# A six-stage transformer kernel: norms by columns, last turns written out, six chunks of five batches in the first expert stage, five carried batches, a count of four products

## The reference

```python
x = x + 0.5 * ffn(layernorm(x))          # weights replaced by alpha * sign(w), gelu between, hidden 512
x = x + gau(layernorm(x))                # gated attention: groups of 32, a quadratic and a linear part
x = x + 0.5 * ffn(layernorm(x))
x = x + 0.5 * moe(layernorm(x))          # 8 experts, top 2, capacity 76 rows per batch and expert
x = x + lin(layernorm(x))                # linear attention, 16 heads of 64, sigmoid gate
x = x + 0.5 * moe(layernorm(x))
```

## Time and profile before

| | us |
|---|---|
| median of three runs | 2459.9 (2459.01 to 2463.73) |
| the profiled execution, its own time | 2451.63 |
| its span | 2449.7 |
| TensorE busy | 2261.4 (92%) |
| VectorE busy | 1594.4 (65%) |
| ScalarE busy | 1306.4 (53%) |
| GpSimd busy | 720.0 (29%) |
| setup, ffn, gau, ffn | 0 to 31.4, to 155.4, to 390.0, to 512.7 |
| moe, lin, moe | to 1063.8, to 1879, to 2449.7 |

### The profile page before, as it was taken

How to read it: one execution, slowest core, us unless ns; L and a number is a source line. 1 busy time by engine, 2 the same in 40 slices (tenths; PEclk the granted TensorE clock), 3 DMA queues, 4 the chain that set the end, 5 groups by cost and what they waited for, 6 DMA issues and landing times.

```text
span 2449.7 us, 48056 instructions
## 1 busy us (share of the span) xinstructions
PE 2261.4 (92%) x14882; PEld 1811.5 (74%) x14882; DVE 1594.4 (65%) x5061; ACT 1306.4 (53%) x2705; POOL 720.0 (29%) x814
## 2 busy tenths in 40 slices
PE   3979998968999999969999999999997889999996
PEld 3969997967766767757778787777776776667676
DVE  5877776776667766566565656565656666676754
ACT  3755555744444444446666666666663444444443
POOL 1202220024547665430000000000000356565654
PEclk9989999989999999999999999999998999999998
DMA  7040000000011111110000000000000001111122
GB/s 256 0 163 0 0 0 0 0 2 18 24 32 42 33 40 37 48 34 0 0 0 0 0 0 0 0 0 0 0 0 0 12 23 36 43 47 48 42 55 73
DMA packets 71011, 67.98 MB, mean 28 GB/s; under 512 B 9712, under 2 KB 58352, under 8 KB 70512
## 3 DMA queue, kind: packets, MB, share of 16 engines
q1 hardware_dynamic: 61648, 47.68, 6.2%
q0 software_dynamic: 8192, 16.79, 3.1%
q10 hardware_dynamic: 1056, 2.10, 0.3%
HBM read 32.47 MB, written 34.08 MB: 27 GB/s over the span
## 4 chain that ended last, share of the span: by engine, by line
PE 49%; DVE 3%; issue 2%; ACT 1%; POOL 0%; DMA 0%; ACTq 0%; POOLq 0%; DVEq 0%
PE moe_bank L1628 6%; PE moe_bank L1614 5%; PE lin_bank L1008 5%; PE moe_bank L1618 5%; PE lin_bank L934 5%; PE lin_bank L942 4%; PE lin_bank L953 4%; PE lin_bank L961 4%; PE lin_bank L984 4%; PE lin_bank L1000 2%; PE moe_bank L1602 2%; PE lin_bank L971 1%; ACT lin_xT L1071 0%; DVE all_x L1455 0%; POOL all_landed L1446 0%
## 5 line engine op out<-in xcount | busy, mean ns | idle before, releaser
L1692 ACT ACTIVATE moe_fc<-moe_bank,all_b_fc 128x380 f32<-128x380 f32 (+2 forms) x512 | 262.8, 513 | 312.6 <-PE moe_bank L1614 299.0
L1804 DVE SCALAR_TENSOR_TENSOR moe_act<-moe_bank,all_b_moe_gate,moe_fc 128x380 f32<-128x380 f32 (+2 forms) x512 | 270.4, 531 | 203.5 <-PE moe_bank L1618 113.3
L1618 PE MATMUL moe_bank<-moe_rowsT,all_w_gate 128*128 128x380 f32 (+2 forms) x1024 | 348.7, 422 | 6.9 <-DVE moe_act L1804 6.9
L1614 PE MATMUL moe_bank<-moe_rowsT,all_w_fc 128*128 128x380 f32 (+2 forms) x1024 | 353.9, 427 | 0.0
L1628 PEld LDWEIGHTS moe_bank<-all_w_proj,moe_act 128*128 128x128 f32 x2688 | 316.7, 193 | 12.4 <-ACT moe_act L1699 1.8
L1628 PE MATMUL moe_bank<-all_w_proj,moe_act 128*128 128x128 f32 x2688 | 324.5, 277 | 1.4 <-ACT moe_act L1699 1.4
L1446 POOL DMA_INDIRECT all_landed<-rows_out,all_take_at x256 | 266.5, 1041 | 128.7 <-issue 126.9
L1618 PEld LDWEIGHTS moe_bank<-moe_rowsT,all_w_gate 128*128 128x128 f32 x1024 | 185.9, 190 | 94.9 <-DVE moe_act L1804 9.6
L1524 POOL TENSOR_SCALAR moe_hot<-all_slot_ids,moe_slot 128x608 bf16<-128x608 f32 x120 | 219.3, 1835 | 85.8 <-issue 51.5
L1171 POOL COPY lin_xn_ones<-lin_xn 128x254 f32<-128x254 f32 x32 | 12.8, 400 | 741.0 <-PE lin_bank L942 737.6
L1699 ACT ACTIVATE moe_act<-moe_act 128x760 f32<-128x760 f32 (+2 forms) x256 | 181.5, 709 | 91.1 <-DVE moe_act L1804 91.0
(11 more groups left out here) (219 smaller groups left out, 4410.8 us busy)
## 6 DMA issues: line engine op xcount, KB each, us to landing
rows_out<-moe_expert_out SPq DMA_DIRECT2D x80, 128.0 KB
rows_out<-all_zeros SPq DMA_DIRECT2D x1, 9728.0 KB, 28.0
rows_out<-moe_expert_out SPq DMA_DIRECT2D x80, 62.0 KB
all_landed<-rows_out,all_take_at POOLq DMA_INDIRECT x256, 2.7
out<-all_x SPq DMA_DIRECT2D x5, 640.0 KB
rows_out<-moe_expert_out SPq DMA_DIRECT2D x48, 64.0 KB
...
```

The source lines that it names most:

```text
L1614: nc.tensor.matmul(bank[FC + j % 2][:, 0:c.width], k.w_fc[:, e, j * P:(j + 1) * P], rowsT[:, c.n % 2, e, 0:c.width], start=True, stop=True ...
L1618: nc.tensor.matmul(bank[GATE + j % 2][:, 0:c.width], k.w_gate[:, e, j * P:(j + 1) * P], rowsT[:, c.n % 2, e, 0:c.width], start=True, stop= ...
L1692: nc.scalar.activation(fc[:, j, 0:c.width], bank[FC + j % 2][:, 0:c.width], ACT.Identity, bias=k.b_fc[:, e * MC + j:e * MC + j + 1]).then_ ...
L1804: nc.vector.scalar_tensor_tensor(act_in[:, i % 2, j, 0:c.width], bank[GATE + j % 2][:, 0:c.width], k.b_moe_gate[:, e * MC + j:e * MC + j + ...
```

## The change

Six parts.

1. Setup: ScalarE issues its two parts of `x` only once the feed-forward weights have landed. VectorE takes the statistics of the first 16 tiles alone.
2. Norms: the form without ScalarE everywhere. The first 8 columns are computed first, then work begins, and the others follow after a few instructions of the stage. In `gau` both roots are computed together, in instructions of twice the width. In the first `ffn` stage the statistics of the other 48 tiles are taken there: 16 of them in the prologue, three in each of the first 12 turns, the last six after those; then follow the remaining 42 columns of the norm.
3. The last four turns of `ffn` and the last two of `gau` are written out without the work past batch 31.
4. The first `moe` stage uses chunks of (2, 5, 5, 5, 5, 5, 5), so chunk 0 routes five batches, at every fourth step. The last stage keeps its chunks and steps.
5. Five batches (27 to 31) are carried into `lin`, all gathered there by GpSimd. The first is combined before turn 0, the others at the ends of turns 0 to 3, which are written out; then 20 columns of the norm, then the loop.
6. `count` is four products instead of seven.

```diff
                 sp.dma_start(w2[:, 0, :], d["w2"]).then_inc(w_in, 16)
                 for i in range(2):
-                    sp.dma_start(k.x[:, 16 * i:16 * i + 16, :], xv[:, 16 * i:16 * i + 16, :]).then_inc(x_in[i], 16)
+                    sp.dma_start(k.x[:, X_PART * i:X_PART * (i + 1), :], xv[:, X_PART * i:X_PART * (i + 1), :]).then_inc(k.x_in[i], 16)
...
+                act.wait_ge(w_in, 48)
                 for i in range(2, 4):
...
-                act.wait_ge(w_in, 48)
...
-                for i in range(4):
-                    dve.wait_ge(x_in[i], 16)
-                    for t in range(16 * i, 16 * i + 16):
-                        last = nc.vector.bn_stats(k.stats[:, t, :], k.x[:, t, :])
+                dve.wait_ge(k.x_in[0], 16)
+                for t in range(X_PART):
+                    last = nc.vector.bn_stats(k.stats[:, t, :], k.x[:, t, :])
...
@@ ffn_stage, VectorE
-                norm.vector(dve)
+                norm.columns(dve, 0, FIRST)
...
+                def raw_stats(lo, n):
+                    for t in range(n):
+                        last = nc.vector.bn_stats(k.stats[:, lo + t, :], k.x[:, lo + t, :])
+                    return last
...
+                def turn(b, s, more=4):
+                    if more >= 4:
+                        normalise(b, 4, s)
+                    if more >= 3:
+                        split_rest(b, 3, 1 - s)
+                    add_out(b)
+                    if more >= 3:
+                        low_part(b, 3, 1 - s)
+                    add_bias(b)
...
                 normalise(0, 3, 1)
-                with dve.Fori(0, BATCHES, 2) as b:
+                norm.columns(dve, FIRST, known)
+                begun = 0
+                if first:
+                    begun = 12
...
+                    with dve.Fori(0, begun, 2) as b:
+                        for s in range(2):
+                            turn(b + s, s)
+                            raw_stats((b + s) * 3 + known, 3)
+                    raw_stats(known + 3 * begun, X_TILES - known - 3 * begun).then_inc(late, 1)
+                    dve.wait_ge(late, 2)
+                    norm.columns(dve, known, X_TILES)
+                with dve.Fori(begun, BATCHES - 4, 2) as b:
...
@@ ffn_stage, TensorE
-                with pe.Fori(0, BATCHES, 2) as b:
+                with pe.Fori(0, BATCHES - 4, 2) as b:
...
+                for b in range(BATCHES - 4, BATCHES):
+                    if b + 1 < BATCHES:
+                        up(b, 1, 1 - b % 2)
+                    if b + 3 < BATCHES:
+                        transpose(b, 3, 1 - b % 2)
+                    down(b, b % 2)
...
@@ gau_stage, VectorE
                 normalise(0, 0)
+                residual_scales(0, FIRST, 2)
+                norm.columns(dve, FIRST, X_TILES)
                 split_heads(0, 0, 0)
...
@@ lin_stage, VectorE
-                for b in k.carried.batches:
-                    k.carried.combine(dve, b, late)
-                norm.columns(dve, k.carried.batches[0] * TILES, X_TILES)
-                with dve.Fori(0, BATCHES - 1) as b:
...
+                early = max(0, len(k.carried.batches) - LANDED)
+                for carried in k.carried.batches[:early]:
+                    k.carried.combine(dve, carried, late)
+                for b, carried in enumerate(k.carried.batches[early:]):
+                    turn(b)
+                    k.carried.combine(dve, carried, late)
+                norm.columns(dve, k.carried.batches[0] * TILES, X_TILES)
+                with dve.Fori(len(k.carried.batches) - early, BATCHES - 1) as b:
+                    turn(b)
...
@@ Carried.gather
         for b in self.not_gathered:
+            if b - LANDED in self.batches:
+                pool.wait_ge(late, 3 * (b - LANDED - self.batches[0]) + 2)
+                pool.nop(nofuse=True)
             self.gather_rows(b)
...
@@ moe_stage
-CHUNKS = (2, 3, 5, 5, 5, 5, 5, 2)
-ROUTE_STEP = (9, 5, 5, 5, 5, 5, 9)
+OWN = 2
+CARRY_CHUNKS = (OWN, 5, 5, 5, 5, 5, 5)
+LAST_CHUNKS = (OWN, 3, 5, 5, 5, 5, 5, 2)
...
+            return 9 if sizes[c.n + 1] == 2 else 4 if sizes[c.n] == OWN and sizes[c.n + 1] == 5 else 5 if c.n else 9
...
-                    for t in range(TILES):
-                        at = COUNTS + t * TKE
...
-                        nc.tensor.matmul(ps, k.tri[:, :], mask[:, b % 2, t, :, :].rearrange("p k e -> p (k e)"), start=True, stop=False)
-                        if t:
-                            nc.tensor.matmul(ps, k.ones[:, :], mask[:, b % 2, t - 1, :, :].rearrange("p k e -> p (k e)"), start=False, stop=False)
-                        for s in range(TILES):
-                            last = nc.tensor.matmul(second, k.ones[:, :], mask[:, b % 2, s, 0, :], start=False, stop=(s == TILES - 1))
+                    ps, m = bank[ROUTE + b % 2][:, COUNTS:COUNTS + TILES * TKE], mask[:, b % 2, :, :, :]
+                    nc.tensor.matmul(ps, k.tri[:, :], m.rearrange("p t k e -> p (t k e)"), start=True, stop=False)
+                    nc.tensor.matmul(ps[:, TKE:], k.ones[:, :], m[:, 0, :, :].rearrange("p k e -> p (k e)"), start=False, stop=False)
+                    second = ps.rearrange("p (t n) -> p t n", t=TILES)[:, :, EXPERTS:]
+                    for t in range(TILES):
+                        last = nc.tensor.matmul(second, k.ones[:, :], m[:, t:t + 1, 0, :].broadcast_to([P, TILES, EXPERTS]),
+                                                start=False, stop=(t == TILES - 1))
```

222 lines of the change are left out of this document (117 added, 105 removed).

## The result

The changed kernel takes 2464.03 us, the median of 20 runs (2461.76 to 2465.95); the kernel before takes 2460.0 in 20 runs beside it (2458.64 to 2463.73). The ratio is 1.0014, with an interval of 1.0007 to 1.0020: no gain, rather a loss of 4 us. The forecast was 2446, its range ended at 2458; it was wrong.

A forecast was written before the change was run, and what follows sets the result against it. TensorE was taken as full in mid-stage, with gains in setup, stage changes, chunk 0 and omitted work. Terms −4.0 + 11.0 − 3.7 − 0.2 − 17.6 − 4.8 + 5.2 = −14.1 from 2459.9 gave 2446 us, range 2433 to 2458.

The forecast's parts named there:

- The new chunk 0 routes five at a step of 4: First moe, chunk 0: five routings at 4.6 us each on 33.0 less 1 give 55 us, bounds 46 and 77.7.
- Rival D: First moe, chunk 0: five routings at a step of 4 don't keep pace with two buffer sets; 77.7, kernel 2469; chance 0.06.
- the forecast's terms for the stage: First moe: 56 units instead of 64 and a wide last unit, −17.6 us; half of the saving in counts, −2.4.
- Counts, −4.8: Both moe stages: three fewer products save 0.08 us at each of 60 batches, −4.8 us, bounds 0 and −6.
- gau, −3.7: gau: earlier start from both roots in one instruction, −2.4 us; last turn, −1.3; bounds −1 and −6.
- First ffn, +11.0: First ffn: start −0.95, norm of 24 columns +2.1, statistics in turns +7.3, stop +4.5, last turns −2.0 us; bounds +4 and +14.
- Rival B: First ffn: VectorE's gaps take the extra statistics, +1.0 us instead of +7.3; kernel 2440; chance 0.17.
- Setup, −4.0: Setup: first part of x lands near 10 and all that follows on SP moves with it; −4.0 us, bounds 0 and −6.
- Rival A: Setup: wins nothing, as SP is held by something other than the landing of x; kernel 2450; chance 0.15.
- Second ffn, −0.2: Second ffn: start −0.9, norm of 66 columns in the prologue +2.7, last turns −2.0 us; bounds −2 and +2.
- lin, +5.2: Start of lin: late copy 4.6, four combines 4.8, norm 3.3, loop entry 0.5 make 13.2 against 8.0 us; bounds +1 and +8.
- Rival C: lin: the combines hide in VectorE's idle time, so their 4.8 us go; kernel 2441; chance 0.10.

## Why the prediction was wrong

**The step that failed** is "The new chunk 0 routes five at a step of 4 ...: 33.0 less 1 for its own start, plus 5 × 4.6 = 55". It took 70.1. I had priced each routing by the price per routing of a chunk in which they stand wider, as if it were work on TensorE, and not asked in what order the parts meet on VectorE at the new step. At lags of 5 (assignment) and 9 (second half of moe_hot) a step of 4 puts the half for one batch into the same slot as the assignment of the next. Rival D had the right place and sign (slower, from 69 on; it came at 70.1) but the wrong reason, sets of buffers, and 0.06. With the order mended and nothing else, the chunk takes 53.9 and the first moe 530.97: the forecast's terms for the stage (551.1 − 17.6 − 2.4) make 531.1. So the arithmetic of 56 units instead of 64 held to within a few us. That it meets to 0.1 is luck: the counts gave nothing, and chunks 0 and 1 came about 1 us under their forecast each. About 15 to 16.5 us are this one step.

**Counts, −4.8: failed.** The premise was that behind a TensorE at 98% each saved product is saved time. The run with seven products shows next to nothing lost with them (0.7 us, within the noise). Busy time that is left out isn't time won as long as gaps of the same size lie beside it.

**gau, −3.7: failed by its other side.** The last turns written out bring 2.5 (1.3 forecast), and the start of the stage about 1.7 (2.4). Against this each of 15 pairs of turns takes 13.75, not 13.47: +4.2, which had no term. What lengthens the pair is not shown. The top of the loop is where to look, as the normalise at 306.28 takes 0.72 and stands behind 0.44 of issue, but with 0.42 of issue the pair was 13.60 in two kernels and 13.70 in a third.

**First ffn, +11.0: sizes.** Read off TensorE's turn starts: start −0.9 (−0.95), norm of 24 columns +1.8 (+2.1), statistics in the turns +6.7 (+7.3), stall +7.2 (+4.5), last turns −1.9 (−2.0); in all +12.9. The pairs take 7.5, not 7.8, so somewhat more hid than I took; but one normalise at 77.81 cost 1.7 more (2.31 for 0.60), with GpSimd on SBUF, and its turn 2.0. (The +7.3 was also not what its own numbers give: 1.46 less 0.32 is 1.14 a pair, 6.8 for six.) The row before had 1.58. The Trainium skill (SBUF — State Buffer, Who interferes with whom) says that an instruction of one engine that holds the shared pair of ports keeps the other out for its whole length; the trace agrees, with 2.31 us from 77.81 on beside GpSimd's instruction of 2.35 that had begun at 77.43. The stall was mis-sized: I had VectorE stopped for 5.6 and TensorE with a microsecond in hand. TensorE has nothing in hand there, waits 5.60 at 101.06 alone, and its turn is 10.5 long instead of 3.3, so 1.6 more lie beside that wait. Rival B (the statistics hide) is refuted.

**Setup, −4.0: −2.35.** Right in its main part: the first part of x landed at 9.35 and the held issue ended at 10.35, where I had about 10 for both. That the one waits for the other is not shown (see the run with x asked for at once). The step that was too large is "all that follows on SP moves with it": the list behind it grew by 2.7 us, from 15.68 to 18.38. Rival A is refuted, by the run with x asked for at once too.

**Second ffn, −0.2.** 124.27 in the profiled run, but 122.62 or 122.63 in ten of the other kernels with the same code there: −0.1.

**lin, +5.2: right**, its mechanisms too, but that the sum meets to 0.1 is luck. Turn 0 took 29.31 and so lost 4.6, as forecast; three turns with a combine took 25.17, +0.47 each where I had 1.2; the turn with the norm of 20 columns, the fourth combine and the loop's entry took 30.58, +5.9 (5.0). That makes 11.9 against the 8.0 of before, +3.9. The missing 1.1 is a later start of turn 0 in the stage (28.56 us against 27.42), and that isn't the change's: with the same lin, the run with a step of 5 has 27.44. Rival C (combines hide) was right for most of three combines of four, and worth 2.2 and not 4.8.

In the sum: chunk 0 +15.1, counts +4.8, gau +3.7, the two ffn stages +3.7, setup +1.7, and the chunks beside chunk 0 gave about 1.5 more than forecast. That is 27.5, which is the +13.4 of the traces less the −14.1; by the medians the miss is 18. The other 9.5 are the favourable execution of before from which the terms were read. For the same reason the 2448.55 of the kernel with the halves ahead lies near the forecast partly by luck: the misses of counts, gau, ffn and setup are all still in it.
